# One stream of 32 heads in the hyperbolic attention stage, with six square roots per turn on ScalarE

## The chip, the cores and the metric

The kernel runs on one core of a Trainium2 chip. The metric is the device time of one execution in microseconds (us). The median of three executions of the kernel before is 6000.16 us (5999.64 to 6000.69).

## The reference, cut to what matters

The program computes four residual layers on x of shape (2, 2048, 256): causal attention, a feed-forward layer with low-rank experts, attention in hyperbolic space, and the same feed-forward layer again. Each first normalizes its input. The change is in the third layer, which has 2 batches x 16 heads of dimension 16:

```python
q_h, k_h, v_h = exp_map_at_origin(x @ W.T, c)      # W_q, W_k, W_v, per head: scaled by tanh of the norm
arg     = maximum(1 + 2c * |q - k|^2 / maximum((1 - c|q|^2)(1 - c|k|^2), EPS), 1 + EPS)
dist    = arccosh(arg) / sqrt(c)                   # log(arg + sqrt(arg^2 - 1))
weights = softmax(-beta * dist - bias)             # over 2048 keys, for 2048 queries
out_tan = weights @ log_map_at_origin(v_h, c)      # then mapped out and back, heads joined, @ W_o.T
```

## The kernel before, in words

The work of one head is cut into 16 chunks of 128 keys by 2048 queries, so there are 32 x 16 = 512 chunks. In this text the *argument* of a chunk is the matrix that stands inside arccosh. A chunk passes five hands:

- **TensorE** (PE) multiplies queries and keys into PSUM, in two halves (`scores`, L1620).
- **VectorE** (DVE) makes the argument from each half (`argument`, L1381, it reads `ra_rep`, one row per head repeated over the partitions), clamps it (`clamp`, L1388) and squares it into a second buffer (`square_by`, L1083). GpSimd (POOL) makes one square of every four.
- **ScalarE** (ACT) takes the root of argument^2 - 1, two chunks in one instruction of 128 x 4096 (`root`, L1520).
- **GpSimd** issues a DMA that adds the argument to the root in place (`sums`, L1095). The *sum* of a chunk is this transfer.
- **ScalarE** takes the logarithm (L1527) and the exponential (L1533) of the sum: the *weights*. **TensorE** then multiplies them with the values (`product`, L1633).

Root needs another function table than logarithm and exponential, so ScalarE works in turns. `BATCHED = 4`: it does the roots of chunks 4n+4 to 4n+7 (two instructions), loads a table, does the weights of 4n to 4n+3, loads a table, and so on. Arguments live in a ring of 7 slots: `argument` of chunk c waits until the sum of chunk c - 7 has landed. Squares, roots and weights share a ring of 10 slots. `product` runs 10 chunks behind `scores` in TensorE's queue.

Before a head can start, its queries and keys are split into bfloat16 parts (`prepare`: part 0, part 1 and part 2, on GpSimd, in its queue between the sums), transposed by TensorE in four groups at the head's chunks 8 to 11 and copied by VectorE (L1394). `take_v` copies the values. SyncE (SP) loads the raw rows and `ra_rep` of the next head.

All of this stands inside a loop over the two batches. Each batch first projects its 16 tiles of 128 tokens, works out the scale factors of all heads, multiplies them in (L1363, on VectorE), runs its 256 chunks, drains them, and multiplies with W_o tile by tile.

Of the kernel before, what the change touches and what calls it, by code (L numbers as in the profile page):

```python
# [10 lines left out]
F32 = mybir.dt.float32  # L11
# [7 lines left out]
P = 128  # L19
# [10 lines left out]
FACTOR_COLS = TB * 16  # L30
# [6 lines left out]
def make_env(nc, ctx):  # L37
# [32 lines left out]
class Norm:  # L70


    STEPS = 7

    def __init__(self, nc, env, name):
# [3 lines left out]
        self.var_done = env.ctx.enter_context(nc.semaphore(f"{name}_var_done"))  # L79
# [5 lines left out]
    def moments(self, dve, a, z, part=0):  # L85
# [858 lines left out]
HB, DB = 16, 16  # L944
GUARD = 1e-5
# [8 lines left out]
NCHK = TB  # L954
HALF = COLS // 2
# [15 lines left out]
def stage_attn_b(nc, env, norm, after, w_qkv, w_o, scalars, ra_scratch, x_scratch, kv_scratch):  # L971

    with ExitStack() as ctx:
# [3 lines left out]
        def sem(n):  # L989
# [4 lines left out]
        tok = tiles[:, 0:6, :].rearrange("p s n -> p (s n)").rearrange("p (a h t d) -> p a h t d", a=3, h=HB, d=DB)  # L994
        out_tok = tiles[:, 2:4, :].rearrange("p s n -> p (s n)").rearrange("p (t d) -> p t d", d=D)
        xnT = tiles[:, 10:10 + KC, :]
        xn = tiles[:, 12, :].rearrange("p (j d) -> p j d", d=D)[:, 0:4, :]
        w_in = tiles[:, 13, 0:KC * 3 * D].rearrange("p (c n) -> p c n", c=KC)
        sq = tiles[:, 6, 0:2 * 3 * D].rearrange("p (j n) -> p j n", j=2)
        osq = tiles[:, 10:12, :].rearrange("p a n -> p (a n)")  # L1000
        oT = tiles[:, 12, 0:2 * D].rearrange("p (j n) -> p j n", j=2)
        wo_sb = tiles[:, 13, 0:KC * D].rearrange("p (c n) -> p c n", c=KC)
# [14 lines left out]
        tmp = tiles[:, 6, :].rearrange("p (i n) -> p i n", n=TB * HB)  # L1017
        nsq = tiles[:, 7, 0:3 * TB * HB].rearrange("p (i n) -> p i n", n=TB * HB)
        ons = tiles[:, 8, 0:3 * TB * HB].rearrange("p (i n) -> p i n", n=TB * HB)
        raT = tiles[:, 9, 0:2 * P].rearrange("p (c k) -> p c k", c=2)  # L1020
# [3 lines left out]
                 "pool_step stack_done grpT_done grp_copied "  # L1024
                 "x_saved x_back tok_done kv_saved k_loaded v_loaded v_ready scores_done scores_read a_ready sq_D sq_P "
                 "root_done sum0 sum1 sum2 sum3 sum4 sum5 sum6 sum7 ln_done w_done av_done "
                 "o_copied oT_done o_done osq_done osum_done oroot_done o_scaled loT_done loT_copied out_done "
                 "x_added gz_done arr_freed").split()
        S = {n: sem(n) for n in names}
        block = ctx.enter_context(nc.Block())  # L1030
# [716 lines left out]
```

## Time and profile before

| | us |
|---|---|
| median of three executions | 6000.16 |
| the profiled execution: time | 6001.92 |
| its span, first to last instruction | 6000.0 |
| the first two layers | 0 to 2370 |
| hyperbolic layer: before the first root, first stream of 256 chunks, the stretch between, second stream, the end | 134, 1601, 165, 1604, 46 |
| the last feed-forward layer | 5919 to 6000 |

ScalarE is busy for 75% of the whole span, VectorE for 78%, TensorE for 67% and GpSimd for 24%. These are averages over layers with different limits, so they don't say which engine sets the time of the streams. The views by stretch and by time that are shown below do.

### The profile page before, as it was taken

The page shows a single profiled execution, that of the slowest core. Times are in us where ns is not written, and L with a number is a line of the kernel's source. Part 1 is how long each engine was busy: PE and PEld are TensorE (multiplying, and loading weights), DVE is VectorE, ACT ScalarE, POOL GpSimd, SP SyncE. Part 2 cuts the span into 40 slices and gives each one's busy share as a digit, 9 for nine tenths or more (in the row PEclk, how much of TensorE's full clock was granted, in tenths as well). Part 3 has the DMA queues.
Part 4 walks back from the last instruction along what each step waited for, and adds up shares of the span by engine and source line. Part 5 has one row for each costly group of instructions (what it writes and reads, how often), then busy time and mean ns, then how long its engine had stood idle before and what let it go on. Part 6 is the DMA issues. An engine that isn't in the chain of part 4 may idle for free. (4 is left out here: it accounts for less than half of the span.)

```text
span 6000.0 us, 69126 instructions
## 1 busy us (share of the span) xinstructions
PE 4044.0 (67%) x22020; PEld 1836.9 (31%) x22020; DVE 4672.1 (78%) x7192; ACT 4511.1 (75%) x3666; POOL 1445.0 (24%) x1219
## 2 busy tenths in 40 slices
PE   8999999999999998444444444445354444444447
PEld 5555555555555555111110101003111111111104
DVE  7666666766666666788989899984889898989875
ACT  4555555555555553399999999995499999999993
POOL 0000000000000000144444444430244444444430
PEclk9999999999999998677777777777566777777767
DMA  1000000000000001388888888884588888888882
GB/s 38 5 5 5 8 5 6 5 5 5 5 5 5 5 2 34 100 179 180 187 180 187 177 186 177 185 173 114 130 186 182 181 187 180 187 180 187 178 172 74
DMA packets 137266, 628.67 MB, mean 105 GB/s; under 512 B 28102, under 2 KB 66184, under 8 KB 66696
## 3 DMA queue, kind: packets, MB, share of 16 engines
q0 software_dynamic: 73728, 536.90, 44.7%
q1 hardware_dynamic: 63112, 86.55, 4.2%
q8 instruction: 211, 3.46, 0.2%
q14 instruction: 215, 1.76, 0.1%
HBM read 65.30 MB, written 21.23 MB: 14 GB/s over the span
## 5 line engine op out<-in xcount | busy, mean ns | idle before, releaser
L1381 DVE SCALAR_TENSOR_TENSOR b_tiles<-b_ra_rep,b_cap,psum 128x1024 f32<-128x1024 f32 x1024 | 1261.1, 1271 | 247.5 <-PE psum L1620 235.0
L674 DVE CUSTOM_DVE_ANT_0 a_srow<-psum,a_bias 128x512 f32<-128x512 f32 (+3 forms) x1280 | 725.7, 607 | 494.2 <-PE psum L855 491.1
L1620 PE MATMUL psum<-b_qT,b_kT 126*128 126x512 bf16 x2048 | 761.4, 482 | 502.6 <-DVE b_tiles L1381 500.2
L733 ACT ACTIVATE a_pT<-psum 128x512 f32<-128x512 f32 (+3 forms) x1056 | 512.1, 527 | 657.1 <-PE psum L867 656.7
L1633 PE MATMUL psum<-b_tiles,b_v_aug 128*32 128x512 f32 x2464 | 447.3, 810 | 680.4 <-ACT b_tiles L1533 680.3
L867 PE MATMUL psum<-ident,a_srow 128*128 128x128 f32 x4352 | 625.8, 280 | 70.5 <-DVE a_pT L547 32.9
L1388 DVE TENSOR_SCALAR b_tiles<-b_tiles 128x2048 f32<-128x2048 f32 x512 | 665.9, 1301 | 5.5
L751 ACT ACTIVATE a_srow<-a_srow,a_nmax 128x1536 f32<-128x1536 f32 (+15 forms) x512 | 610.5, 1198 | 23.1 <-DVE a_nmax L680 21.2
L855 PE MATMUL psum<-a_k,a_q 64*128 64x512 f32 (+3 forms) x2560 | 623.5, 572 | 0.0
L1633 PE MATMUL psum<-X,b_v_aug 128*32 128x512 f32 x1632 | 295.8, 809 | 443.3 <-ACT X L1533 443.3
L1533 ACT ACTIVATE b_tiles<-b_tiles,b_sc 128x4096 f32<-128x4096 f32 x154 | 585.6, 3802 | 5.1
L867 PEld LDWEIGHTS psum<-ident,a_srow 128*128 128x128 f32 x4352 | 475.5, 141 | 321.0 <-issue 151.8
L1520 ACT ACTIVATE b_tiles<-b_tiles 128x4096 f32<-128x4096 f32 x154 | 552.7, 3613 | 25.8 <-DVE b_tiles L1083 24.9
L1527 ACT ACTIVATE b_tiles<-b_tiles 128x4096 f32<-128x4096 f32 x154 | 555.9, 3610 | 0.9
L885 PE MATMUL psum<-a_pT,a_v 128*64 128x256 f32 (+1 forms) x4608 | 541.3, 374 | 14.8 <-ACT a_pT L733 10.8
L1083 DVE TENSOR_TENSOR b_tiles<-b_tiles 128x2048 f32<-128x2048 f32 x232 | 536.2, 2311 | 0.6
L1620 PEld LDWEIGHTS psum<-b_qT,b_kT 126*128 126x128 bf16 x2048 | 156.2, 108 | 1239.7 <-DVE b_tiles L1381 949.2
L1083 POOL TENSOR_TENSOR b_tiles<-b_tiles 128x2048 f32<-128x2048 f32 x76 | 273.4, 3597 | 653.8 <-PE psum L1633 644.4
L653 DVE TENSOR_SCALAR a_srow<-a_srow,a_zinv 128x1536 f32<-128x1536 f32 (+15 forms) x512 | 404.9, 791 | 18.2
L885 PEld LDWEIGHTS psum<-a_pT,a_v 128*64 128x64 f32 x4608 | 311.8, 136 | 284.4 <-issue 172.3
L1520 ACT ACTIVATE X<-X 128x4096 f32<-128x4096 f32 x102 | 366.7, 3612 | 38.5 <-DVE X L1083 38.0
L1533 ACT ACTIVATE X<-X,b_sc 128x4096 f32<-128x4096 f32 x102 | 387.8, 3802 | 3.4
(208 smaller groups left out, 5504.4 us busy)
## 6 DMA issues: line engine op xcount, KB each, us to landing
b_tiles<-b_tiles POOLq DMA_DIRECT2D x308, 1024.0 KB, 12.5
X<-b_tiles POOLq DMA_DIRECT2D x204, 1024.0 KB, 13.0
b_ra_rep<-ra_scratch SPq DMA_DIRECT2D x32, 1024.0 KB, 6.7
x_scratch<-X SPq DMA_DIRECT2D x8, 1024.0 KB, 10.5
kv_scratch<-b_tiles SPq DMA_DIRECT2D x4, 2048.0 KB, 8.5
X<-x_scratch SPq DMA_DIRECT2D x8, 1024.0 KB, 9.5
X<-in_x_dram SPq DMA_DIRECT2D x8, 512.0 KB, 6.8
a_wqk<-in_wqk_dram SPq DMA_DIRECT2D x32, 128.0 KB, 2.6
```

The lines of the kernel that those rows point to most:

```text
L674: nc.vector.tensor_tensor_reduce(out=srow[:, n % ROWS, h, a:z], in0=bank(c % 2 * 2 + h, 0, z - a), in1=bias[:, h, off + a:off + z], scale= ...
L751: nc.scalar.activation(row, row, ACT.Exp, bias=nmax[:, n, h:h + 1], accum_out=zsum[:, n, h:h + 1]).then_inc(exp_done, 1)
L855: nc.tensor.matmul(bank(c % 2 * 2 + h, 0, z - a), q_sb[rows(h), tiles[n] * P:(tiles[n] + 1) * P], k_sb[rows(h), a:z], start=True, stop=Tru ...
L867: last = nc.tensor.transpose(bank(T_BANKS[e % 3], (jt - a) * P, (jt - a + 1) * P), srow[:, n % ROWS, h, jt * P:(jt + 1) * P], env.ident[:, :])
L885: last = nc.tensor.matmul(bank(6, lo, IB)[rows(h), :], v_sb[:, jt, rows(h)], pT[:, h, jt, lo:IB], start=(jt == 0), stop=(jt == 2 * ib + 1) ...
L1083: engine.tensor_tensor(y_slot(h, k), a, a, ALU.mult).then_inc(S["sq_" + name], 1)
L1381: nc.vector.scalar_tensor_tensor(out=a[:, s * HALF:(s + 1) * HALF], in0=ra_rep[:, j, s * HALF:(s + 1) * HALF], scalar=cap[:, j, k:k + 1], ...
L1388: nc.vector.tensor_scalar(a, a, 1.0, 1.0 + GUARD, ALU.add, ALU.max).then_inc(S["a_ready"], 1)
L1520: nc.scalar.activation(y, y, ACT.Sqrt, bias=-1.0).then_inc(S["root_done"], 1)
L1533: nc.scalar.activation(y, y, ACT.Exp, bias=col(SHIFT), scale=col(NEG_S)).then_inc(S["w_done"], 1)
L1620: last = nc.tensor.matmul(half_ps(s)[:, i * BANK:(i + 1) * BANK], kT[:, j, k * P:(k + 1) * P], qT[:, j, cs], start=True, stop=True)
L1633: last = nc.tensor.matmul(bank(4 + j)[32 * i:32 * i + 32, :], v_aug[:, j, k, :], y_slot(h, k)[:, i * BANK:(i + 1) * BANK], start=(k == 0), ...
```

## The change

The loop over the batches is taken apart. Both batches are projected first (32 tiles), the rows of all 32 heads go to DRAM (`row_scratch`), and one stream of 512 chunks follows; each head's output goes to DRAM too (`o_scratch`) and is loaded again for one common end. The multiplication with the scale factors moves from VectorE to GpSimd. ScalarE's turns become six chunks long, and the last two chunks of a turn keep their weights for the next turn. The second ring has 12 slots in place of 10, the ring of arguments still 7.

```diff
-BATCHED = 4
-SQUARES = "DDPD" * 4
-A_SLOTS = [6, 7, 8, 9, 14, 2, 5]
-Y_SLOTS = [10, 11, 12, 13, 15, 16, 17, 18, 3, 4]
+ROOTS, KEPT = 6, 2
+WIDE = 2
+SQUARES = "DDPD"
+A_SLOTS = [12, 4, 5, 14, 13, 10, 11]
+Y_SLOTS = [17, 18, 0, 1, 2, 3, 6, 7, 8, 9, 15, 16]
-V_LAG = 10
+V_LAG = 12
+NO_POOL = len(Y_SLOTS)
...
+        root_batches = [(c, min(c + ROOTS, CHUNKS)) for c in range(0, CHUNKS, ROOTS)]
...
+            weighted = 0
+            for a, z in root_batches:
+                for c in range(a, z, WIDE):
+                    root(c)
+                upto = z - KEPT if z < CHUNKS else CHUNKS
+                if upto > weighted:
+                    nc.scalar.preload_act_table_set("natural_log_exp_and_others")
+                for c in range(weighted, upto, WIDE):
+                    weight(c)
+                weighted = max(weighted, upto)
```

GpSimd's queue, new. `todo` holds the parts of the next heads with the chunk from which they are due:

```diff
+            scale(0)
+            pool.wait_ge(S["tok_scaled"], 3)
+            for part in range(3):
+                prepare(pool, nc.gpsimd, 0, part)
+            take_v(pool, nc.gpsimd, 0)
+            for part in range(3):
+                prepare(pool, nc.gpsimd, 1, part)
+            scale(1)
...
+                if g + 2 < HEADS:
+                    todo += [(g * NCHK + 4 * n + 8, "prepare", g + 2, n) for n in range(3)]
+                if g + 1 < HEADS:
+                    todo += [(g * NCHK + 12, "v", g + 1, 0)]
...
+            squares(*root_batches[0])
+            for n, (a, z) in enumerate(root_batches):
+                sums(a, z)
+                if n + 1 < len(root_batches):
+                    squares(*root_batches[n + 1])
+                while todo and todo[0][0] <= z:
+                    _, what, g, part = todo.pop(0)
+                    if what == "v":
+                        take_v(pool, nc.gpsimd, g)
+                    else:
+                        prepare(pool, nc.gpsimd, g, part)
```

SyncE's queue per head, new. `load_qk` waits until `prepare` of the head before is complete:

```diff
+            def load_qk(g):
+                sp.wait_ge(S["pool_step"], g * PREP)
+                sp.dma_start(qk_raw[:, :], of_head(g, 0, ROW_V)).then_inc(S["qk_loaded"], 16)
...
+            for g in range(2, HEADS):
+                load_qk(g)
+                load_v(g)
+                if g >= 3:
+                    store_o(g - 3)
+                load_ra(g)
```

VectorE's queue, where the factors of the first batch stand among the tiles of the second, and where a slot of `tiles` waits for what it held (`row_saved1` is the DRAM copy of the second batch's rows):

```diff
+            for n in range(NT + 4):
+                if n < NT:
+                    normalize(n)
+                if n == 11:
+                    scalars_of()
+                if n == TB + 4:
+                    factors(0)
+                if n % 4 == 3 and n >= 7:
+                    for m in range(n - 7, n - 3):
+                        square_norms(m // TB, m % TB)
+                if n == TB + 3:
+                    lengths(0)
...
+            def first_use(slot):
+                if slot < 6:
+                    dve.wait_ge(S["row_saved0"], 64)
+                    dve.wait_ge(S["v_ready"], 1)
+                elif slot < 12:
+                    dve.wait_ge(S["row_saved1"], 64)
```

The queue of ScalarE at the start of a stream, before: a turn has two root instructions (L1520) and two pairs of logarithm (L1527) and exponential (L1533). `X` and `b_tiles` are the two places in which the ring's slots lie.

```order
L1520 ACT_TABLE_LOAD
L1520 ACTIVATE b_tiles<-b_tiles 128x4096
L1520 ACTIVATE X<-X 128x4096
L1541 ACT_TABLE_LOAD
L1527 ACTIVATE b_tiles<-b_tiles 128x4096
L1533 ACTIVATE b_tiles<-b_tiles,b_sc 128x4096
L1527 ACTIVATE b_tiles<-b_tiles 128x4096
L1533 ACTIVATE b_tiles<-b_tiles,b_sc 128x4096
```

ScalarE's queue in the changed kernel, a few turns into the stream. The lines are those of the new file: L1618 root, L1624 logarithm, L1626 exponential.

```order
L1618 ACT_TABLE_LOAD
L1618 ACTIVATE b_tiles<-b_tiles 128x4096 x2
L1618 ACTIVATE X<-X 128x4096
L1634 ACT_TABLE_LOAD
L1624 ACTIVATE b_tiles<-b_tiles 128x4096
L1626 ACTIVATE b_tiles<-b_tiles,b_sc 128x4096
L1624 ACTIVATE b_tiles<-b_tiles 128x4096
L1626 ACTIVATE b_tiles<-b_tiles,b_sc 128x4096
L1624 ACTIVATE b_tiles<-b_tiles 128x4096
L1626 ACTIVATE b_tiles<-b_tiles,b_sc 128x4096
```

Two table loads now stand around three roots and three pairs, where they stood around two and two.

GpSimd's queue before, in the fourth turn of a head: the square (L1083), then part 2 of `prepare` (from L1151 to the last L1119), then the four sums (L1095).

```order
L1083 TENSOR_TENSOR b_tiles<-b_tiles 128x2048
L1151 COPY b_cap<-shared 128x16
L1119 CAST b_stack<-b_aug 128x16x2x18
L1119 CAST b_stack<-b_aug 128x16x36
L1123 TENSOR_TENSOR b_aug<-b_aug,b_stack 128x288 x2
L1119 CAST b_stack<-b_aug 128x16x2x18 x2
L1095 DMA X<-b_tiles 128x2048 x2
L1095 DMA b_tiles<-b_tiles 128x2048 x2
```

GpSimd's queue in the changed kernel, after the sums of chunks 12 to 17. L1088 is the square, L1147 to L1118 are part 2 of `prepare`, L1295 the sums of chunks 18 to 23.

```order
L1088 TENSOR_TENSOR b_tiles<-b_tiles 128x2048
L1088 TENSOR_TENSOR X<-b_tiles 128x2048
L1147 COPY b_cap<-b_qk_raw 128x16
L1118 CAST b_stack<-b_aug 128x16x2x18
L1118 CAST b_stack<-b_aug 128x16x36
L1122 TENSOR_TENSOR b_aug<-b_aug,b_stack 128x288 x2
L1118 CAST b_stack<-b_aug 128x16x2x18 x2
L1295 DMA b_tiles<-b_tiles 128x2048 x4
L1295 DMA X<-b_tiles 128x2048 x2
```

In this turn two squares, those of chunks 18 and 22, stand ahead of part 2, and part 2 stands ahead of six sums.

## Rows read from the trace of the kernel before

**Rows 1.** Stretch: length, busy us of PE, PEld, DVE, ACT, POOL, clock, DMA share, GB/s.

```profile
3000.00:3196.40 196.40, 94.81 (x453) 20.47 (x452) 176.57 (x140) 194.03 (x65) 89.55 (x76) 0.71 0.88 183
```

**Rows 2.** ScalarE in order of time, one turn of the stream: start, duration, operation.

```profile
3198.99 1.28 ACT L1520 ACT_TABLE_LOAD   x1
...
3207.42 1.28 ACT L1541 ACT_TABLE_LOAD   x1
...
3223.53 1.28 ACT L1520 ACT_TABLE_LOAD   x1
```

**Rows 3.** DMA in 785.6 us of the stream (3000 to 3785.6), by queue.

```profile
q0 software_dynamic: 18240, 132.84, 84.5%
q1 hardware_dynamic: 3456, 10.49, 3.6%
```

**Rows 4.** Same stretch: landing of the sums; `ra_rep` loads (count, KB, us to landing).

```profile
DMA to landing us min/median/max: 7.0/13.0/22.1
...
b_ra_rep<-ra_scratch SPq DMA_DIRECT2D x8, 1024.0 KB, 7.2
```

**Rows 5.** VectorE in order of time, stream.

```profile
3204.91 2.46 DVE L1381 SCALAR_TENSOR_TENSOR b_tiles<-b_ra_rep,b_cap,psum 128x1024 f32<-128x1024 f32 x2
3207.29 2.28 DVE L1083 TENSOR_TENSOR X<-b_tiles 128x2048 f32<-128x2048 f32 x1
...
3210.62 2.46 DVE L1381 SCALAR_TENSOR_TENSOR b_tiles<-b_ra_rep,b_cap,psum 128x1024 f32<-128x1024 f32 x2
...
3219.23 2.47 DVE L1381 SCALAR_TENSOR_TENSOR b_tiles<-b_ra_rep,b_cap,psum 128x1024 f32<-128x1024 f32 x2 [2.81 <-PE psum L1620]
...
3222.94 2.46 DVE L1381 SCALAR_TENSOR_TENSOR b_tiles<-b_ra_rep,b_cap,psum 128x1024 f32<-128x1024 f32 x2
...
3228.66 0.68 DVE L1394 COPY b_qT<-psum 126x1024 bf16<-126x1024 bf16 x1
```

**Rows 6.** GpSimd in order of time: part 2, a square, `take_v` and part 1.

```profile
3197.34 1.19 POOL L1151 COPY b_cap<-shared 128x16 f32<-128x16 f32 x1
...
3201.29 4.22 POOL L1119 CAST b_stack<-b_aug 128x576 bf16<-128x576 f32 x2
...
3218.34 3.60 POOL L1083 TENSOR_TENSOR b_tiles<-b_tiles 128x2048 f32<-128x2048 f32 x1 [6.63 <-PE psum L1633]
...
3271.78 1.38 POOL L1170 COPY b_v_aug<-b_v_raw 128x256 f32<-128x256 f32 x1
...
3277.02 1.40 POOL L1123 TENSOR_TENSOR b_aug<-b_aug,b_stack 128x288 f32<-128x288 f32 x2
```

**Rows 7.** Ahead of the first stream: ScalarE, then VectorE.

```profile
2439.17 1.28 ACT L1506 ACT_TABLE_LOAD   x1
...
2443.28 3.35 DVE L1345 RECIPROCAL b_tiles<-b_tiles 128x512 f32<-128x512 f32 x1 [1.06 <-ACT b_tiles L1508]
...
2457.28 13.34 DVE L1363 TENSOR_TENSOR b_tiles<-b_tiles 128x4096 f32<-128x4096 f32 x3
...
2487.26 2.47 DVE L1381 SCALAR_TENSOR_TENSOR b_tiles<-b_ra_rep,b_cap,psum 128x1024 f32<-128x1024 f32 x2 [6.33 <-DMA b_ra_rep<-ra_scratch]
```

**Rows 8.** ScalarE between and after the streams.

```profile
4105.15 1.28 ACT L1557 ACT_TABLE_LOAD   x1
...
4144.53 0.38 ACT L1562 ACTIVATE b_tiles<-psum 128x256 f32<-128x256 f32 x1 [0.70 <-PE psum L1677]
...
4171.12 1.08 ACT L1493 ACTIVATE b_tiles<-psum 128x512 f32<-128x512 f32 x2 [2.10 <-PE psum L1574]
...
4185.06 1.09 ACT L1493 ACTIVATE b_tiles<-psum 128x512 f32<-128x512 f32 x2 [2.10 <-PE psum L1574]
...
5873.25 1.28 ACT L1557 ACT_TABLE_LOAD   x1
...
5918.94 0.32 ACT L108 ACTIVATE shared<-shared,ln_eps 128x32 f32<-128x32 f32 x1 [4.84 <-DVE shared L100]
```

**Rows 9.** The page's DMA issues: count, KB each, us to landing.

```profile
kv_scratch<-b_tiles SPq DMA_DIRECT2D x4, 2048.0 KB, 8.5
```

More of the change, by code:

```diff
@@ L944 @@
 HB, DB = 16, 16
+HEADS = BATCH * HB
 GUARD = 1e-5
@@ L1016, in stage_attn_b @@
         NS_Q, E_K, EN_K, CAP_K = range(4)
[L1017 to L1020, printed above, removed]
+        NF = TB * HB
+        tok = [tiles[:, 6 * b:6 * b + 6, :].rearrange("p s n -> p (s n)").rearrange(
+            "p (a h t d) -> p a h t d", a=3, h=HB, d=DB) for b in range(BATCH)]
@@ new lines, in _, with squares, sums @@
+            scale(0)
[6 more added lines that the diff above has]
+            scale(1)
+            def squares(a, z):
+                for c in range(a, z):
+                    square_by(pool, nc.gpsimd, "P", c)
+            def sums(a, z):
+                for c in range(a, z):
+                    pool.wait_ge(S["root_done"], pairs_to(c))
+                    nc.gpsimd.dma_start(y_slot(c), a_slot(c), accum_op=ALU.add).then_inc(S[f"sum{c % 8}"], 16)
@@ L1258, in _ @@
+            assert not todo
+            pool.wait_ge(S["o_ready"], 1)
+            scale_out(nc.gpsimd, 1).then_inc(S["o_scaled1"], 1)
         @block.vector
@@ new lines, in _ @@
+            dve.wait_ge(S["o_loaded0"], 16)
+            out_scale(HEADS - 1)
+            dve.wait_ge(S["o_done"], HEADS * 4)
+            o_scales(0)
+            scale_out(nc.vector, 0).then_inc(S["o_scaled0"], 1)
+            o_factors(1)
+            o_scales(1)
+            dve.sem_inc(S["o_ready"], 1)
+            for t in range(NT):
+                dve.wait_ge(S["out_done"], t + 1)
+                dve.wait_ge(x_back[t * 4 // NT], 16)
+                xt = env.X[:, t, :]
+                nc.vector.tensor_tensor(xt, bank(2 + t % 2, 0, D), xt, ALU.add).then_inc(S["x_added"], 1)
+                dve.wait_ge(S["x_added"], t + 1)
+                after.sums(t)
@@ new lines, in _ @@
+            transpose_out(0)
+            for t in range(NT):
+                if t + 1 < NT:
+                    transpose_out(t + 1)
+                pe.wait_ge(S["loT_copied"], t + 1)
+                if t >= 2:
+                    pe.wait_ge(S["x_added"], t - 1)
+                for c in range(KC):
+                    last = nc.tensor.matmul(bank(2 + t % 2, 0, D), oT[:, t % 2, c * P:(c + 1) * P], wo_sb[:, c, :],
+                                            start=(c == 0), stop=(c == KC - 1))
+                last.then_inc(S["out_done"], 1)
```

865 lines of the change are left out of this document (428 added, 437 removed).

## The prediction

> **What bounds the kernel now.** I read the windows of one stream first, then ScalarE by time, then the engines that feed it, and last the two edges of the layer.
>
> In the stream ScalarE is busy for 194.03 of 196.4 us, 99%. VectorE has 176.57 (90%), the 16 DMA engines a share of 0.88, TensorE 94.81, GpSimd 89.55 [rows 1]. So ScalarE sets the time, and VectorE and the DMA engines stand close behind. One turn of four chunks is 3223.53 - 3198.99 = 24.54 us: 7.15 for two roots, 14.83 for two pairs of weights, 2.56 for two table loads [rows 2]. 24.54/4 is 6.13 us a chunk. Outside the streams ScalarE has little to do: from the end of the first at 4105.15 to the first root of the second, 165 us pass.
>
> **What the change does to a turn, if nothing waits.** Per four chunks 24.54 - 2.56 = 21.98 us are work. Six chunks: 21.98 x 1.5 + 2.56 = 35.5 us, 5.92 a chunk. For 512 chunks that is 110 us less. ScalarE starts its next instruction 1.28 to 1.30 us after a load begins [rows 2], so 85 fewer pairs of loads of 1.28 give these 110 us at most. The Trainium skill ("ScalarE: Activation LUTs", What ACT_TABLE_LOAD costs) adds a drain of about 1.38 us to each switch, which would make the saving over 220 us. The trace shows no such gap, and I go by the trace.
>
> **What a longer turn asks of the others.** Let T be the start of a turn's first root, and count chunks from the turn's first, 0. Roots end at T+3.6, 7.1, 10.7. Three pairs of weights start at 12.0, 19.4, 26.8; the next turn's roots start at 35.5, its third root is due at 42.6. The first pair of weights belongs to the last turn and is ready; the third needs the sums of chunks 0 to 3.
>
> - *Sums.* A sum that finds the DMA idle lands 7.0 us after its issue [rows 4], 10.9 after T with 0.3 us for the issue. The next follow at the DMA's rate: 84.5% of 24.54 us for four sums [rows 3, 2] is 5.2 us each. Landings: 10.9, 16.1, 21.3, 26.5, 31.7, 36.9. The third weights are due at 26.8 and have their sums at 26.5: a margin of 0.3 us, where a turn of four had one of many.
> - *The ring of arguments.* It still has 7 slots, so the argument of chunk 7 waits for sum 0 at 10.9, chunk 12's for sum 5 at 36.9. A chunk takes VectorE 3210.62 - 3204.91 = 5.7 us, or 3222.94 - 3219.23 = 3.7 where GpSimd squares [rows 5]. The square of chunk 11 follows the argument of chunk 12 and is done 2.4 + 2.3 = 4.7 us after that starts [rows 5]. One long chain: 10.9, 16.6, 22.3, 26.5 (sum 3), 32.2, 37.9, square done at 42.6, due at 42.6. No margin in turns where GpSimd makes one square. Where it makes two, it ends at 41.6: 1.0. A head adds four copies of 0.7 at its chunks 8 to 11 and one more at 13.
> - *GpSimd.* The order of instructions alternates: one square in a turn (of chunk 8), two in the next (6 and 10). The later one can start when chunk 10 is clamped, 27.5 + 5.7 = 33.2, and takes 3.6: 36.8. Then come the due parts, and only then the next sums, wanted at 35.5 + 3.8 = 39.3. Part 2 costs 3201.29 + 4.22 - 3197.34 = 8.2, `take_v` with part 1 6.6 [rows 6]; part 0 fits. In turns with one square GpSimd is free at 22.3 + 3.6 = 25.9.
>
> Three heads are eight turns. I walk them through by these times; the same order returns every 48 chunks:
>
> 1. *Part 2 after chunks 12 to 17 (two squares).* It ends at 36.8 + 8.2 = 45.0, sums 5.7 late. ScalarE waits 26.5 + 5.7 - 26.8 = 5.4 for the third weights, then, with three copies and one output copy (2.7), 42.6 + 5.7 + 2.7 - (42.6 + 5.4) = 3.0 for the third root.
> 2. *Part 1 after chunks 24 to 29 (two squares).* It ends at 43.4; the turn was lengthened by the 3.0 just counted, so sums are wanted at 42.3: 1.1 late, 0.8 wait.
> 3. *Part 2 after chunks 30 to 35 (one square).* It ends at 34.1, but TensorE wants this head's parts beside chunk 10, which VectorE leaves at 32.2. With transposes and copy (0.7 each) chunk 11 starts at 35.5, 3.3 late; with one more copy the third root waits 4.0.
> 4. *Parts 1 and 2 after chunks 42 to 47.* 25.9 + 6.6 + 8.2 = 40.7, 1.4 late: 1.1 for the weights, then with four copies 41.6 + 1.4 + 2.7 - 43.7 = 2.0.
>
> Sum: 5.4 + 3.0 + 0.8 + 4.0 + 1.1 + 2.0 = 16.3 us in 8 x 35.5 = 284.0. So a chunk costs 300.3/48 = **6.26 us**, more than today's 6.13. The bounds are 5.92 (no wait) and, with the collision below, 6.40. TensorE covers: `product` runs 12 behind, and the argument that starts at 37.9 is 9 ahead of the last weights done, so it is never last.
>
> **The edges.** I place them by time.
> - Projection ends at 2439.17 for batch 0, as now. Then VectorE does `factors(0)` from 2443.28 to 2457.28 (all of it ahead of the scaling [rows 7]) and has three normalizations to do before TensorE gets its next tiles; with their transposes and copies the flow resumes near 2461. Four tiles take 4185.06 - 4171.12 = 13.94 [rows 8]; sixteen end at 2515.
> - `factors(1)` takes 18 us (2439.17 to 2457.28), the first head's four groups about 4 more (my estimate: four copies of 0.7 and the transposes between): first argument at 2537 (before, 2487.26 [rows 7]).
> - The sixth argument's slot needs batch 1's rows in DRAM: from 2535 on GpSimd does parts 1 and 2 (5.2 + 8.2) and `scale(1)`, three products of 4096 columns at twice its 3.6, and the last store of 2 MB takes 8.5 [rows 9]: 2580. In the flow of 5.7 a chunk it would start at 2565.5, so 15 us show. Here VectorE paid 13.34 for scaling; that leaves its queue.
> - From there by the same chains: third root of turn 0 over at 2594, turn 1 starts at 2612, its last square is at 2628, turn 2 starts at 2656. The stream ends 83 turns and 19.7 us (a root, a load, two pairs) later: 2675.7 + 498p, p the us per chunk.
> - After it, 5918.94 - 5873.25 = 45.7 today, and 16 more tiles of 0.38 + 0.70 = 1.08 [rows 8]: 63.
>
> End of the layer: 2738.7 + 498p, against 5918.9. With p = 6.26 it is 5856.2, 62.7 us earlier. The profiled execution took 6001.92; less 62.7 that is 5939. The median of the runs shown is 1.8 us below it: **5937**. In other words, the single stream alone (p = 6.13) gives 127 us, and the longer turn takes half of it back. The kernels are level at p = 6.39, that is when ScalarE waits 2.8 us a turn; I count 2.0.
>
> **The rivals.**
> - *A. ScalarE waits hardly at all.* For it: all my waits are small differences of large times, each under 6 us; parts on GpSimd may run faster while VectorE stands. Against: the argument ring gives no margin by the rows. p = 5.92 gives 498 x 0.34 = 169 less: 5768.
> - *B. SyncE's loads fall on the sums.* `load_qk` waits for part 2, and `ra_rep` follows it. Today that load finds the DMA idle, 7.2 us to landing. In places 1 and 4 part 2 ends just ahead of late sums. The queue's traffic is 3.6% of 785.6 us over 8 heads, 3.5 a head [rows 3], so up to 7.0 per 48 chunks are added, p = 6.40: 6007. The Trainium skill ("DMA: Bandwidth & Descriptors", SWDGE vs HWDGE vs iDMA) says an engine takes turns between the two kinds of queue, which would spread this load over several sums and still delay the fourth. No row here shows the two together.
> - *C. Slower: VectorE's chain decides every turn.* If a chunk costs it 5.9 in place of 5.7, as when GpSimd works beside it, the six steps from sum 0 to the square of chunk 11 end 1.2 later and the third root waits in every turn, one-square turns without margin first. It decides once the wait is above 2.8 a turn; 2.0 + 1.2 = 3.2 gives p = 6.45, 5937 + 498 x 0.19 = 6032.
> - *The stream is not one.* If batch 1's rows came late into the ring, a stall of up to 30 us would stand in front; it is in the range.
>
> **How the numbers follow.** My case, p from 6.1 to 6.35 (5857 to 5982): 0.48. A, below that: 0.22. B, within 15 us of before: 0.14. C: 0.16. Two runs can be told apart from 0.2%, 12 us. Faster by more: my case and A, 0.70; within: 0.12; slower: 0.18. The range for 8 in 10 leaves out the lower part of A and the upper of C: 5800 to 6030.
>
> **What would show it.** ScalarE's busy share in the stream falls from 99% to 94 to 95%, and its idle time stands ahead of the third root of a turn (released by VectorE's square) and ahead of logarithms (released by a sum). A turn without waits is 35.5 us. VectorE's idle time moves from "TensorE" to the DMA's sums. In turns with two GpSimd squares followed by part 2 the sums start over 3 us after the root. There is one first root, near 2555, and ScalarE's last weights end near 5793. I am wrong if ScalarE is at 98% (A), if the sums beside `ra_rep` land over 25 us after issue (B), or if every turn has a wait for a square (C).

## The result, and the profile after it

| kernel | median us | lowest to highest | runs |
|---|---|---|---|
| before | 5999.90 | 5994.64 to 6000.69 | 4 |
| changed | 6072.98 | 6064.94 to 6078.62 | 4 |

The ratio is 1.0123, with a 95% interval of 1.0105 to 1.0140: the change costs 73 us. The profiled execution took 6064.94 us, its span is 6063.1. For that execution the prediction was 5939.

**The stream.** First the windows of a long stretch in the middle of it (columns as in [rows 1]), then the groups of instructions in that stretch, each with busy us, mean ns, and the idle time ahead of it with its releasers:

```profile
3000.00:5400.00 2400.00, 1372.32 (x5286) 249.06 (x5288) 2175.20 (x1622) 2190.72 (x682) 1063.10 (x884) 0.66 0.86 178
```

```profile
L1445 DVE SCALAR_TENSOR_TENSOR b_tiles<-b_ra_rep,b_cap,psum 128x1024 f32<-128x1024 f32 x742 | 913.5, 1271 | 193.7 <-DMA b_tiles<-b_tiles 133.9 <-DMA X<-b_tiles 57.4 <-PE psum L1715 1.9
L1452 DVE TENSOR_SCALAR b_tiles<-b_tiles 128x2048 f32<-128x2048 f32 x371 | 575.8, 1552 | 3.2
L1088 DVE TENSOR_TENSOR b_tiles<-b_tiles 128x2048 f32<-128x2048 f32 x186 | 447.9, 2408 | 0.0
L1624 ACT ACTIVATE b_tiles<-b_tiles 128x4096 f32<-128x4096 f32 x124 | 447.7, 3610 | 78.0 <-DMA b_tiles<-b_tiles 77.6
L1618 ACT ACTIVATE b_tiles<-b_tiles 128x4096 f32<-128x4096 f32 x124 | 444.7, 3610 | 84.7 <-DVE b_tiles L1088 84.0
L1088 POOL TENSOR_TENSOR b_tiles<-b_tiles 128x2048 f32<-128x2048 f32 x62 | 239.4, 3862 | 359.1 <-DVE b_tiles L1452 359.1
L1618 ACT ACTIVATE X<-X 128x4096 f32<-128x4096 f32 x62 | 224.2, 3616 | 37.8 <-DVE X L1088 37.5
```

ScalarE is busy for 91% where it was 99% [rows 1], and each instruction of it is as long as before. Of the 209 us that are missing 199 are waits: 121.5 ahead of roots, released by VectorE's squares, and 77.6 ahead of logarithms, released by sums. The clamp, one line of VectorE (L1452), takes 1552 ns in the mean, though the same instruction takes 1.21 us when it runs alone. The granted TensorE clock is 0.66 in the stretch, where it was 0.71 [rows 1], but VectorE waits for TensorE only 1.9 us there, so the slower clock is not what costs the time.

**The turns.** ScalarE in order of time, a turn with almost no wait, then the worst one:

```profile
3302.51 1.28 ACT L1618 ACT_TABLE_LOAD   x1
...
3307.33 7.30 ACT L1618 ACTIVATE b_tiles<-b_tiles 128x4096 f32<-128x4096 f32 x2
...
3338.10 1.28 ACT L1618 ACT_TABLE_LOAD   x1
...
3349.81 3.62 ACT L1618 ACTIVATE X<-X 128x4096 f32<-128x4096 f32 x1 [3.29 <-DVE X L1088]
...
3366.09 3.62 ACT L1624 ACTIVATE b_tiles<-b_tiles 128x4096 f32<-128x4096 f32 x1 [3.90 <-DMA b_tiles<-b_tiles]
...
3375.82 3.62 ACT L1624 ACTIVATE b_tiles<-b_tiles 128x4096 f32<-128x4096 f32 x1 [2.28 <-DMA b_tiles<-b_tiles]
...
3383.29 1.28 ACT L1618 ACT_TABLE_LOAD   x1
```

The first turn is 3338.10 - 3302.51 = 35.6 us, as predicted without waits; the second is 45.2. All turns read this way, the same pattern returns every eight. Mean waits of turns 2 to 83 by their place in the eight (10 or 11 turns each), worked out from ScalarE's rows:

```
turn mod 8        0     1     2     3     4     5     6     7    sum
third root      2.5   3.0   0.2   1.7   3.1   0.3   5.1   0.0   15.8
logarithm       0.3   0.0   0.2   5.5   0.0   2.9   0.0   0.3    9.1
predicted       1.1   2.0   0     5.4   3.0   0.8   4.0   0     16.3
```

24.9 us in eight turns are 0.52 a chunk, so p = 5.92 + 0.52 = 6.44. The ends of the stream say the same: the first root of turn 2 starts at 2684.76 and that of the last turn at 5893.73, 3208.97/498 = 6.44.

**The port.** VectorE, then GpSimd, in order of time, first in the stream (the first two fences) and then ahead of it (the other two):

```profile
3317.61 5.28 DVE L1452 TENSOR_SCALAR b_tiles<-b_tiles 128x2048 f32<-128x2048 f32 x1
...
3327.40 1.21 DVE L1452 TENSOR_SCALAR b_tiles<-b_tiles 128x2048 f32<-128x2048 f32 x1
```

```profile
3317.31 0.86 POOL L1295 DMA_DIRECT2D b_tiles<-b_tiles  x1 [1.53 <-issue]
3317.88 3.92 POOL L1088 TENSOR_TENSOR b_tiles<-b_tiles 128x2048 f32<-128x2048 f32 x1
```

```profile
2461.00 21.72 DVE L106 TENSOR_SCALAR b_tiles<-X,ln_mean,ln_rstd 128x256 f32<-128x256 f32 x3
...
2567.04 8.19 DVE L1452 TENSOR_SCALAR b_tiles<-b_tiles 128x2048 f32<-128x2048 f32 x1
...
2609.18 2.47 DVE L1445 SCALAR_TENSOR_TENSOR b_tiles<-b_ra_rep,b_cap,psum 128x1024 f32<-128x1024 f32 x2 [5.21 <-DMA row_scratch<-b_tiles]
```

```profile
2461.05 21.52 POOL L1276 TENSOR_TENSOR b_tiles<-b_tiles,X 128x4096 f32<-128x4096 f32 x3 [89.38 <-DVEq L1413]
...
2565.22 26.23 POOL L1276 TENSOR_TENSOR b_tiles<-b_tiles,X 128x4096 f32<-128x4096 f32 x3 [0.24 <-POOL b_stack L1118]
```

A clamp of 1.21 us takes 5.28 when a square of GpSimd runs beside it: the square ends at 3321.8 and the clamp at 3322.9, 1.1 us later, which is nearly all of its own length. Three normalizations, of 0.4 us where one stands alone, take 21.72 beside GpSimd's three products that scale batch 0 (21.52), so each of them lasts as long as one product. So VectorE stands until GpSimd's instruction is over. The Trainium skill ("SBUF — State Buffer", SBUF: two separate sides) states this: the two engines share a pair of ports, and the lock on it is exclusive and held for a whole instruction. The trace agrees, with 5.28 us against 1.21. VectorE's instructions that read PSUM (L1445) stay at 1271 ns.

Over the stretch the port's price can be read off the groups: (1552 - 1210) ns x 371 clamps are 127 us, and squares at 2408 and 2338 ns against 2280 some 29 more: 0.42 us for each of 371 chunks, 2.5 us a turn. By the same sum the kernel before paid 0.11. Taken one by one, the 78 clamps that overlap a square of GpSimd last 2525 ns in the mean and carry 102 of the 127 us; the 193 with nothing of GpSimd's beside them last 1215.

In the kernel before there were as many squares of GpSimd per chunk, and 68 clamps of the same stretch overlap one, but they last only 1316 ns in the mean. The page's group of those squares shows why they rarely fell on the body of a clamp:

```profile
L1083 POOL TENSOR_TENSOR b_tiles<-b_tiles 128x2048 f32<-128x2048 f32 x76 | 273.4, 3597 | 653.8 <-PE psum L1633 644.4
```

There a square waited for a product that freed its slot, and ran while VectorE waited or made arguments from PSUM, as the one at 3218.34 [rows 6] does beside the argument at 3219.23 [rows 5]. In the changed kernel it is released by the clamp (359.1 of 359.1 us above), so it runs into what VectorE does next.

### The profile page after: what moved, and what is told of

Read it like the earlier page. It is cut to its first block and busy times, and to the rows that moved or that the text cites. A ratio compares the mean times of both kernels' runs of the same rounds, so it can differ in the third digit from the quotient of the medians.

```text
span 6063.1 us, 69116 instructions
## 1 busy us (share of the span) xinstructions
PE 4370.5 (72%) x22020; PEld 1842.8 (30%) x22020; DVE 4810.2 (79%) x7142; ACT 4412.5 (73%) x3586; POOL 1518.5 (25%) x1259
## 5 line engine op out<-in xcount | busy, mean ns | idle before, releaser
L1715 PE MATMUL psum<-b_qT,b_kT 126*128 126x512 bf16 x2048 | 906.3, 541 | 1262.8 <-DVE b_tiles L1445 1258.5
L1445 DVE SCALAR_TENSOR_TENSOR b_tiles<-b_ra_rep,b_cap,psum 128x1024 f32<-128x1024 f32 x1024 | 1260.7, 1270 | 261.2 <-DMA b_tiles<-b_tiles 170.0
L1452 DVE TENSOR_SCALAR b_tiles<-b_tiles 128x2048 f32<-128x2048 f32 x512 | 808.3, 1579 | 4.3
L1618 ACT ACTIVATE b_tiles<-b_tiles 128x4096 f32<-128x4096 f32 x171 | 613.1, 3610 | 136.4 <-DVE b_tiles L1088 135.6
L1624 ACT ACTIVATE b_tiles<-b_tiles 128x4096 f32<-128x4096 f32 x171 | 617.3, 3610 | 103.6 <-DMA b_tiles<-b_tiles 102.9
L1626 ACT ACTIVATE b_tiles<-b_tiles,b_sc 128x4096 f32<-128x4096 f32 x171 | 650.1, 3802 | 5.7
L1088 DVE TENSOR_TENSOR b_tiles<-b_tiles 128x2048 f32<-128x2048 f32 x258 | 618.5, 2397 | 0.0
L1728 PE MATMUL psum<-b_tiles,b_v_aug 128*32 128x512 f32 x2736 | 597.9, 966 | 23.8 <-ACT b_tiles L1626 23.8
L1088 POOL TENSOR_TENSOR b_tiles<-b_tiles 128x2048 f32<-128x2048 f32 x84 | 325.2, 3872 | 475.6 <-DVE b_tiles L1452 475.6
L1295 POOL DMA_DIRECT2D b_tiles<-b_tiles x342 | 323.5, 1138 | 356.6 <-ACT b_tiles L1618 342.5
L1618 ACT ACTIVATE X<-X 128x4096 f32<-128x4096 f32 x85 | 307.3, 3616 | 60.0 <-DVE X L1088 59.5
L1626 ACT ACTIVATE X<-X,b_sc 128x4096 f32<-128x4096 f32 x85 | 323.1, 3802 | 2.8
```

Of the source, the lines that this page charges most:

```text
L1088: engine.tensor_tensor(y_slot(c), a, a, ALU.mult).then_inc(S["sq_" + name], 1)
L1445: nc.vector.scalar_tensor_tensor(out=a[:, s * HALF:(s + 1) * HALF], in0=ra_rep[:, j, s * HALF:(s + 1) * HALF], scalar=cap[:, j, k:k + 1], ...
L1452: nc.vector.tensor_scalar(a, a, 1.0, 1.0 + GUARD, ALU.add, ALU.max).then_inc(S["a_ready"], 1)
L1618: nc.scalar.activation(y, y, ACT.Sqrt, bias=-1.0).then_inc(S["root_done"], 1)
L1624: nc.scalar.activation(y, y, ACT.Ln).then_inc(S["ln_done"], 1)
L1626: nc.scalar.activation(y, y, ACT.Exp, bias=col(SHIFT), scale=col(NEG_S)).then_inc(S["w_done"], 1)
```

## The experiments

"Stretch" is 3000 to 5400 us, as above. Each ratio is to runs of the kernel before on the same chip, with its 95% interval. Where two kernels are less than some 10 us apart, their intervals overlap, and the difference alone shows nothing. Diffs are against the changed kernel, if nothing else is said. The waits and means that no line shows are worked out from the same traces.

**1. The turn of four in the single stream** (which part of the change costs the time).

```diff
-ROOTS, KEPT = 6, 2
+ROOTS, KEPT = 4, 4
```

> The changed kernel with ROOTS, KEPT = 4, 4: the single stream stays, ScalarE's turn is as before. Theory (the longer turn of six is what costs): no waits, 24.5 us a turn, 6.14 us a chunk in place of 6.44, about 150 us below the changed kernel, near 5915 to 5930. Rival (the single stream itself, its DRAM traffic or GpSimd's new order costs): it stays above 6000.

Measured: 5901.21 us (5899.59 to 5905.65), ratio 0.9835 (0.9819 to 0.9851). Windows of the stretch, then the clamp:

```profile
3000.00:5400.00 2400.00, 1448.72 (x5588) 262.27 (x5588) 2176.13 (x1712) 2387.86 (x783) 1033.24 (x928) 0.67 0.90 187
```

```profile
L1445 DVE SCALAR_TENSOR_TENSOR b_tiles<-b_ra_rep,b_cap,psum 128x1024 f32<-128x1024 f32 x782 | 964.7, 1274 | 219.7 <-DMA b_tiles<-b_tiles 149.8 <-DMA X<-b_tiles 69.2 <-POOL b_stack L1118 0.3
L1452 DVE TENSOR_SCALAR b_tiles<-b_tiles 128x2048 f32<-128x2048 f32 x392 | 511.5, 1305 | 3.4
```

The time is 14 us below the range, and the rival is out. ScalarE is busy for 99.5% and waits for nothing. The single stream alone gains 99 us, the longer turn loses 172. And the clamp costs 1305 ns with the same work on GpSimd: clamps lose (1305 - 1210) x 392 = 37 us of the stretch at the port, where they lost 127. It is where GpSimd's squares fall in time that makes them dear, not how many there are: here they mostly follow its own sums (it waits 45 us of the stretch for clamps ahead of them, and 889 in the changed kernel), and the 56 clamps that overlap one last 1642 ns.

**2. GpSimd's parts ahead of the next turn's squares** (late sums). In GpSimd's loop:

```diff
                 sums(a, z)
-                if n + 1 < len(root_batches):
-                    squares(*root_batches[n + 1])
                 while todo and todo[0][0] <= z:
                     ...
+                if n + 1 < len(root_batches):
+                    squares(*root_batches[n + 1])
```

> GpSimd does the due parts of prepare ahead of the next squares, so that they stand in the time in which it waits for VectorE's clamp, and no sum is late. Theory G (late sums cause the waits): ScalarE's waits for sums (29 of 786 us) go, and some of those for squares: 100 to 180 us faster, near 5900 to 5970. Theory V (VectorE's chain through the ring of seven arguments, slowed by GpSimd's work on the shared port): less than 60 us faster, waits ahead of the third root stay at 30 to 40 of 786 us.

Measured: 5965.84 us (5960.29 to 5967.50), ratio 0.9944 (0.9928 to 0.9961). In the stretch:

```profile
L1452 DVE TENSOR_SCALAR b_tiles<-b_tiles 128x2048 f32<-128x2048 f32 x385 | 581.6, 1511 | 3.3
L1624 ACT ACTIVATE b_tiles<-b_tiles 128x4096 f32<-128x4096 f32 x128 | 461.8, 3607 | 9.1 <-DMA b_tiles<-b_tiles 8.4
L1618 ACT ACTIVATE b_tiles<-b_tiles 128x4096 f32<-128x4096 f32 x128 | 459.0, 3610 | 83.4 <-DVE b_tiles L1088 83.1
```

The time is in the range of theory G, but the waits for squares are those of theory V. Waits for sums fall from 77.6 to 8.4 us, those for squares stay (121.5, now 113.4). The first sum of a turn is issued 0.31 us after its root in the mean, where it was 2.05 us and up to 9.4. So sums that queue behind parts on GpSimd cost 107 us of the whole, and the other half of the waits is a cause of its own. The port takes even more than before, 0.49 us a chunk, because 32 squares of VectorE now overlap one of GpSimd's, where 15 did.

**3. Nine argument slots, ten for weights** (the ring).

```diff
-A_SLOTS = [12, 4, 5, 14, 13, 10, 11]
-Y_SLOTS = [17, 18, 0, 1, 2, 3, 6, 7, 8, 9, 15, 16]
+A_SLOTS = [12, 4, 5, 14, 13, 10, 11, 8, 9]
+Y_SLOTS = [17, 18, 0, 1, 2, 3, 6, 7, 15, 16]
-V_LAG = 12
+V_LAG = 10
```

> Nine slots for arguments and ten for squares (TensorE's lag 10), in place of seven and twelve. Theory V: VectorE no longer waits for a sum before the argument, the waits for the third root go, those for sums stay: 6.2 us a chunk, 100 to 140 us faster, near 5935 to 5970. Theory G alone: within 30 us of the changed kernel. If the second ring becomes the limit it is not faster.

Measured: 6023.51 us (6019.96 to 6028.39), ratio 1.0039 (1.0024 to 1.0053). No argument waits for a sum any more, but TensorE's products, which now follow ten chunks behind, wait for weights (they waited for nothing in the changed kernel), and the scores behind them:

```profile
L1728 PE MATMUL psum<-b_tiles,b_v_aug 128*32 128x512 f32 x1796 | 351.1, 867 | 354.3 <-ACT b_tiles L1626 354.2
L1445 DVE SCALAR_TENSOR_TENSOR b_tiles<-b_ra_rep,b_cap,psum 128x1024 f32<-128x1024 f32 x752 | 926.1, 1271 | 143.8 <-PE psum L1715 143.7
```

That is half of what theory V gave and more than theory G allowed. The ring helps by 49 us, but the slots taken from the weights turn part of its wait into one for TensorE.

**4. Short loads of `ra_rep`** (rival B). From head 2 on 16 of 2048 columns are loaded, so the scores are not the reference's.

```diff
-sp.dma_start(ra_rep[:, g % 2, :], src.to_broadcast([P, SEQ]))
+sp.dma_start(ra_rep[:, g % 2, 0:16], src[:, 0:16].to_broadcast([P, 16]))
```

> From head 2 on the load of ra_rep brings 16 columns in place of 2048, so the output is not the reference's; the queue and its waits are unchanged, 1 MB of DMA per head is gone. Theory L (SyncE's load beside the sums delays them): 3.5 us for two heads of three, 50 to 110 us faster. Rival (the load is hidden or harmless): less than 15 us.

Measured: 6075.94 us (6062.46 to 6079.93), ratio 1.0129 (1.0112 to 1.0146), the time of the changed kernel; waits for logarithms are 81.1 us in the stretch. Rival B's mark, sums that land over 25 us after issue, was met all the same: 41 of 370 sums of the changed kernel do, up to 32.2 us. But only 7 of them have a load of `ra_rep` beside them, and with the short loads there are 42. All 41 are the fifth or sixth sum of a turn, behind the others of the burst. So `ra_rep` is not the cause; the smaller load of `load_qk` (288 KB) stayed as it was.

**5. Scaling on GpSimd in pieces of 512 columns** (the port ahead of the stream). Each of the six products becomes eight.

```diff
-nc.gpsimd.tensor_tensor(dst, dst, f, ALU.mult)
+for m in range(8): ...
+    nc.gpsimd.tensor_tensor(dst, dst, f, ALU.mult)   # 128x512
```

> The changed kernel with one edit: each of GpSimd's six products that scale the tokens by their factors is issued as eight products of 512 columns in place of one of 4096. In the changed kernel three of VectorE's normalizations that start at 2461.00 end 21.72 us later, beside three whole products of GpSimd (2461.05, 21.52 us), and two clamps of 8.19 and a square of 6.87 us stand beside the second three. Theory lock: an instruction of GpSimd keeps VectorE out of a shared port for its whole length. (The Trainium skill, SBUF - State Buffer, section on the two sides, says so: an exclusive lock held for the whole instruction.) Then VectorE gets in between pieces of some 0.9 us: the projection resumes by about 2468 in place of 2483.5, the clamps fall under 3 us, and the time is 15 to 30 us below 6073: 6043 to 6058. Theory bandwidth: both engines share a rate and the size of a piece makes no difference: the three normalizations still end together near 2482, and the time stays within 8 us of 6073.

Measured: 6081.27 us (6079.88 to 6083.51), ratio 1.0135 (1.0118 to 1.0152). VectorE in order of time:

```profile
2465.07 3.38 DVE L106 TENSOR_SCALAR b_tiles<-X,ln_mean,ln_rstd 128x256 f32<-128x256 f32 x3
...
2563.10 2.46 DVE L1449 SCALAR_TENSOR_TENSOR b_tiles<-b_ra_rep,b_cap,psum 128x1024 f32<-128x1024 f32 x2
2565.48 2.79 DVE L1089 TENSOR_TENSOR X<-b_tiles 128x2048 f32<-128x2048 f32 x1
2568.20 2.08 DVE L1456 TENSOR_SCALAR b_tiles<-b_tiles 128x2048 f32<-128x2048 f32 x1
...
2623.38 2.47 DVE L1449 SCALAR_TENSOR_TENSOR b_tiles<-b_ra_rep,b_cap,psum 128x1024 f32<-128x1024 f32 x2 [38.92 <-DMA row_scratch<-b_tiles]
```

The lock is as the theory has it: three normalizations take 3.38 us in place of 21.72, clamps 2.08 in place of 8.19. The time is no better all the same: 8 us more, at the edge of the second range, with intervals that overlap. GpSimd gets batch 1 scaled at 2595.5 in place of 2591.5 (its three products cost 36.24 us in pieces, 26.23 whole), and the sixth argument waits for the last store of these rows, 14 us later than before. Most of those 14 us are the store itself. It is issued at 2595.5 together with four sums, which GpSimd could not issue while it scaled, and lands after 27.9 us; in the changed kernel two sums were beside it, and it took 17.7. The store ahead of it, with no sum beside it, took 7.5 in both. The same edit with the turn of four:

> The single stream with the turn of four (5901.21) and the scaling in eight pieces. The edge is the same as with the turn of six, and ScalarE has no waits in the stream, so what the pieces save there (15 to 30 us by the lock) should show in full: 5870 to 5886. If the start of the stream is bound by the rows of batch 1 through DRAM and not by VectorE, 5893 to 5902.

Measured: 5906.64 us (5905.65 to 5911.12), ratio 0.9847 (0.9830 to 0.9863). Nothing is gained here either; it is 5 us above the range for a start that is bound by the rows. So the stream starts when batch 1's rows are in DRAM, not when VectorE is ready.

**6. Batch 1 scaled on VectorE, turn of four.**

```diff
-            scale(1)                      # GpSimd
+            for i in SCALED[1]: ...       # VectorE, right behind factors(1)
+                nc.vector.tensor_tensor(dst, dst, f, ALU.mult)
```

> The single stream with the turn of four (5901.21), and VectorE, not GpSimd, makes the three products that scale batch 1, right after its factors. In the changed kernel GpSimd's three end at 2591.45 and the sixth argument waits for the store of the rows until 2609.18. On VectorE they would end near 2568, the first argument moves from 2558 to about 2572, the rows land near 2577, and the sixth argument starts near 2600. If the rows of batch 1 are what the start of the stream waits for, 5889 to 5897; if the first argument is, 5910 to 5918.

Measured: 5893.43 us (5884.22 to 5895.41), ratio 0.9826 (0.9809 to 0.9842). That is in the first range, and 8 us below experiment 1, with intervals that overlap. VectorE takes 13.10 us for the three products, GpSimd took 26.23, and no argument waits for the rows:

```profile
2546.50 13.10 DVE L1440 TENSOR_TENSOR b_tiles<-b_tiles,X 128x4096 f32<-128x4096 f32 x3 [0.24 <-DVEq L1412]
```

**7. Short squares on GpSimd** (port against ring). On top of experiment 2, GpSimd squares 128 of 2048 columns from chunk 96 on, and the roots there take no 1 off; the output is not the reference's. All waits and transfers stay.

```diff
-engine.tensor_tensor(y_slot(c), a, a, ALU.mult)
+w = 128 if name == "P" and c >= 96 else 2048
+engine.tensor_tensor(y_slot(c)[:, 0:w], a[:, 0:w], a[:, 0:w], ALU.mult)
```

> The kernel with the parts put ahead of the next squares on GpSimd (5965.84 us), with one more edit: from chunk 96 on GpSimd squares 128 of a chunk's 2048 columns, and the roots take no 1 off (so that they stay real), which changes the output. All waits, transfers and every instruction of VectorE, ScalarE and TensorE stay. It asks whether the third root waits because GpSimd's squares slow VectorE, or because seven slots for arguments make the chain too long by themselves. Theory lock: clamps, at 1511 ns in the mean, fall below 1300 and squares from 2.5 to under 2.4 us; that is 0.3 us and more a chunk in a chain of six, so of the 113 us of waits for squares in 2400 us at least 60 go, and the time is 5850 to 5905. Theory ring: the chain has no margin without that too: the waits for squares stay above 80 us in 2400, and the time is 5935 to 5970.

Measured: 5907.54 us (5905.60 to 5912.81), ratio 0.9845 (0.9828 to 0.9861). In the stretch:

```profile
L1453 DVE TENSOR_SCALAR b_tiles<-b_tiles 128x2048 f32<-128x2048 f32 x392 | 514.5, 1313 | 3.3
L1619 ACT ACTIVATE b_tiles<-b_tiles 128x4096 f32<-128x4096 f32 x130 | 466.0, 3609 | 59.9 <-DVE b_tiles L1089 59.5
L1619 ACT ACTIVATE X<-X 128x4096 f32<-128x4096 f32 x65 | 234.8, 3612 | 9.2 <-DVE X L1089 8.8
```

The clamp falls from 1511 to 1313 ns, waits for squares from 113.4 to 68.3, the time by 58 us. The time is 3 us above the range of the theory with the port and 27 below the other, but the waits lie between the two: the port is 45 of these 113 us, and the chain has too little margin with most of it gone too (0.18 us a chunk are left of 0.49). Shorter squares did not bring the sums forward: the first of a turn is issued 0.31 us after its root in both kernels.

**8. Two squares a turn on GpSimd**, on top of experiment 2.

```diff
-SQUARES = "DDPD"
+SQUARES = "DDPDPD"
```

> The turn of six with parts first (5965.84 us), and GpSimd squares two chunks of every turn (the third and the fifth) in place of one and two in turns. VectorE has 2.3 us less to do in every second turn, and its chain is the same in all turns. If the chain is decided by how many squares VectorE makes, waits for squares fall from 113 us in 2400 to under 90 and the time is 5930 to 5955. If GpSimd's squares cost VectorE at the port what they take off it, the time is within 12 us of 5966; clamps rise above 1511 ns in either case.

Measured: 5916.69 us (5914.97 to 5919.75), ratio 0.9865 (0.9848 to 0.9881), a bigger gain (49 us) than either theory gave. Waits for squares fall to 73.1 us though clamps rise to 1642 ns. One square less in the chain is worth more than the port takes.

**9. Both edits of 7 and 8 together** (output as in 7).

> The turn of six with parts first and two squares a turn on GpSimd (5916.69), of which GpSimd makes 128 of 2048 columns from chunk 96 on, and roots without the 1 taken off; the output is changed. It asks how much of the 73 us of waits for squares in 2400 us is the port and how much the length of the chain. Theory port: clamps fall from 1642 to 1300 ns, six times 0.34 us come off each turn, the waits for squares are under 20 us and the time is 5855 to 5880. Theory chain: VectorE's chain has no margin even with two squares fewer and no port: waits stay above 50 us and the time is 5895 to 5915.

Measured: 5884.56 us (5874.34 to 5891.36), ratio 0.9815 (0.9800 to 0.9830). Waits for squares are 40.0 us in the stretch and those for sums 21.4. It lies between the two theories again: the time is nearer to the one with the port (5 us above its range), the waits to the other.

**10. More work on VectorE, in the turn of six and in that of four.** After each clamp, with a wait between, its lower bound is taken once more on 256 columns. The first run is on top of experiment 2, the second on experiment 1.

```diff
-nc.vector.tensor_scalar(a, a, 1.0, 1.0 + GUARD, ALU.add, ALU.max).then_inc(S["a_ready"], 1)
+link(nc.vector.tensor_scalar(a, a, 1.0, 1.0 + GUARD, ALU.add, ALU.max))
+nc.vector.tensor_scalar(a[:, 0:256], a[:, 0:256], 1.0 + GUARD, None, ALU.max).then_inc(S["a_ready"], 1)
```

> The turn of six with parts first (5965.84) and one more instruction of VectorE for each chunk: the clamp's lower bound once more on 256 of 2048 columns, with a wait between the two, 0.2 to 0.3 us by a row of 0.23 us for such a size. The result is unchanged. VectorE was busy for 2281.93 of 2400 us there by the profile's count. Theory chain: six steps in a row decide each turn, so each of 85 turns gets 1.2 to 1.8 us longer: 6065 to 6120. Theory rate: the sums through DMA set when arguments start, and VectorE has room between them: under 30 us more, 5966 to 5996.

> The same extra instruction for each chunk in the single stream with the turn of four (5901.21), where ScalarE waits for nothing. If only the longer turn made VectorE's chain decide, there is room for it: within 15 us, 5896 to 5916. If VectorE is at its bound there too, 0.2 to 0.3 us a chunk on 512 chunks show: 5990 to 6050.

Measured: 6041.57 us (6033.15 to 6044.82) in the turn of six, 76 more than without; 5909.55 (5908.89 to 5911.75) in that of four, 8 more. The added instruction's group in the turn of six, then the windows and that group in the turn of four:

```profile
L1454 DVE TENSOR_SCALAR b_tiles<-b_tiles 128x256 f32<-128x256 f32 x375 | 156.8, 418 | 12.8
```

```profile
3000.00:5400.00 2400.00, 1491.44 (x5590) 263.78 (x5590) 2362.06 (x2106) 2387.73 (x783) 1068.50 (x928) 0.65 0.90 187
```

```profile
L1454 DVE TENSOR_SCALAR b_tiles<-b_tiles 128x256 f32<-128x256 f32 x392 | 131.4, 335 | 13.4
```

In the turn of four 0.34 us a chunk on VectorE are nearly free, as the first range had it: ScalarE is still busy for 2387.73 us. In the turn of six 0.42 x 512 = 214 us of work show as 76. That misses both of my ranges: VectorE had room for about two thirds of it. But VectorE is now busy for 2359.91 of 2400 us, 98%, so its whole work may set the time there, and this run cannot tell that from a chain that decides in part of the turns. The same instructions take VectorE 6.29 us a chunk in the turn of six and 6.03 in that of four (2359.91/375 and 2362.06/392).

**11. The best of each turn.** The turn of six with experiments 2, 6 and 8, against experiment 6 once more. A version with 2, 3 and 5 together came before it.

> The turn of six with three edits at once: parts ahead of squares on GpSimd, nine slots for arguments and ten for weights with the product ten chunks behind, and scaling in eight pieces. Parts first alone was 5965.84, nine slots alone 6023.51 against 6073. If the late sums and the argument ring are separate causes, the gains add: 6073 - 107 - 49, and 15 to 30 less at the start of the stream: 5890 to 5905. If the second slot pair only moves the wait to the weights' slots (TensorE's product waited for weights with ten of them), the ring gives little on top: 5930 to 5950.

> The turn of six with all that helped: parts first, two squares a turn on GpSimd (together 5916.69) and batch 1 scaled on VectorE, which gave 7.8 us with the turn of four. The edge is the same, so 5905 to 5912. The turn of four with that scaling is 5893; the turn of six would only be level with it if fewer waits for squares came out of the better start, 5890 to 5897.

> The turn of four with batch 1 scaled on VectorE once more, beside the best turn of six on the same chip: 5889 to 5897 as before, 10 to 18 us under the best turn of six.

| kernel | median us | lowest to highest | ratio and interval |
|---|---|---|---|
| six: 2, 3, 5 | 5958.66 | 5956.21 to 5962.84 | 0.9931 (0.9915 to 0.9948) |
| six: 2, 6, 8 | 5899.80 | 5894.63 to 5909.20 | 0.9834 (0.9820 to 0.9847) |
| four: 6 | 5891.52 | 5887.36 to 5894.53 | 0.9821 (0.9808 to 0.9835) |

The first is above both of its ranges: the nine slots give at most 7 us beside experiment 2 and not 49, though pieces may cost some there (experiment 5). Clamps are 1411 ns, and arguments wait 130.7 us for TensorE. The second lies between its ranges. The last two, on one chip, are 8 us apart where I expected 10 to 18, with intervals that overlap. The turn of four with its 1.28 us loads is not slower than the best turn of six that I found, and it is 1.8% faster than the kernel before.

## Why the prediction was wrong

It forecast 5937, and 5800 to 6030; 6072.98 is outside, and on the other side of before. In the profiled execution 126 us are to be explained. They are 3209.0 - 6.26 x 498 = 91.5 in the stream, 2684.8 - 2656 = 29 at its start, and 5.5 behind it.

- **"Six chunks: 35.5 us"** holds: turns without waits take 35.5, a load 1.28, and ScalarE starts its next instruction 1.28 to 1.30 us after the load begins. The prediction's "85 fewer pairs of loads" is a slip: it is 85 fewer loads (128 turns become 86), and 85 x 1.28 gives the 110 us.
- **"The single stream alone gives 127"** was right in kind: 99 in experiment 1. Of the missing 28 the start of the stream, below, accounts for all: it is 29 late.
- **Place 1** (part 2 after chunks 12 to 17) was right: 5.4 and 3.0 predicted, 5.5 and 3.1 measured. **Place 3** had 4.0, measured 5.1. **Place 2** had 0.8, measured 2.9. **Place 4** had 1.1 and 2.0; 0.3 and 3.0 were measured, and 2.5 at the third root before it. The turn ahead of place 1 waits 1.7 where I had nothing. Experiment 2 shows that the places are what I said they are, late sums behind parts: 107 us.
- **The step that failed is the size of VectorE's chunk: "A chunk takes VectorE 5.7 us, or 3.7 where GpSimd squares".** Both were read off a turn in which only the last 0.2 us of a square of GpSimd fell on a clamp. The change releases those squares by the clamp, and so the clamps and squares of one chunk cost VectorE 0.42 us more in the mean, 2.5 in a turn with no margin. Experiment 7 takes most of it away and gains 58 us. It also shows that this is not all: with most of the port's cost gone, and sums in time, 68 us of waits for squares stay in 2400. The chain of six steps from sum 0, 42.6 us against 42.6, had no room for copies and transposes in turns that I had booked at nothing; that these are the rest is argued, no run shows it.
- **Rival C** comes out in its number: p = 6.45 for 6.44, "3.2 us a turn" for 3.1 (24.9/8). With the 35 us of the two edges its 6032 would be near 6067, and the median is 6073. In part that is luck. The chunk costs 0.42 us more and not 0.2, which by its sum would be 2.0 + 2.5 = 4.5 us a turn, and its wait does not stand in every turn: turns 2 and 7 of eight have under 0.4 us. It had 0.16.
- **The start.** "The flow resumes near 2461" was 2483: three normalizations stood behind GpSimd's scaling of batch 0, which I had costed at nothing for VectorE. The first argument came at 2558 for 2537, the sixth at 2609 for 2580. Experiments 5 and 6 show that what decides there is when batch 1's rows are stored: freeing VectorE gave nothing, and scaling on the faster engine brought the sixth argument to 2591 and the time down by 8 us, within the noise. The store of these rows took 17.7 us where I had 8.5, beside two sums.
- **Rival B** did not happen, as far as `ra_rep` goes (experiment 4), and there is no stall of 30 us between batches: once turn 2 runs the longest turn is 45.2 us.
- My marks were ScalarE at 94 to 95% (it is at 91), a first root near 2555 (2585.8) and VectorE waiting for sums in place of TensorE (it does, 191 of 194 us).

What stays open: how the 68 us that are left in experiment 7 divide among the ring, the copies, the rest of the port's cost and the place where TensorE wants its parts. Nine slots without taking two from the weights were not tried: the 19 slots are all in use.

## What to carry to other kernels

A longer turn saves what it saves on one engine and takes the room from all that feed it. Walk the chain with each engine's duration beside the others' work, not with that of a quiet moment: the group's mean against its shortest instance (here 1552 against 1210 ns) says how much it pays for its neighbour. Look for that pair of numbers before an edit brings two engines' bursts together. And split a change of two parts in two: one part here gained 99 us and the other lost 172.

## What the runs showed of the hardware

- VectorE's clamps, squares and normalizations, which read and write SBUF (the on-chip memory of tiles) alone, stand while an instruction of GpSimd runs: a clamp took 5.28 us for 1.21, 8.19 beside products of 4096 columns, 2.08 beside products of 512. Its instructions that read PSUM (L1445) took 1270 to 1276 ns in the mean in every kernel here.
- Cutting GpSimd's product in eight made it dearer while VectorE worked beside it: 36.24 us for three in place of 26.23. With little beside it, it was 24.56 in place of 21.52 (batch 0).
- A broadcast load of 1 MB on SyncE's queue beside the sums cost nothing measurable (6075.94 without nearly all of it, 6072.98 with it). A store of 2 MB on the same queue, for which VectorE waited, landed 7.5 us after issue with no sum beside it, 17.7 beside two and 27.9 beside four.
- Function table loads of ScalarE took 1.28 us each, and its next instruction started 1.28 to 1.30 us after the load began.
